# Two edits of a float32 post-norm transformer layer on one core: where ScalarE's copies of turned blocks stand beside its exponentials, and a 64-row feed-forward tile laid out over the whole TensorE array

## The chip, the cores and the metric

The kernel runs on one NeuronCore of one Trainium2 chip. The number that counts is the device time of one execution in microseconds (us). A core has five engines that run side by side, each through its own instruction list: PE (TensorE), DVE (VectorE), ACT (ScalarE), POOL (GpSimd) and SP (SyncE). They meet at semaphores that the kernel counts up and waits for by hand. There is no scheduler: the order of each engine's list is the order of the Python calls.

## The reference, cut to what matters

```python
B, T, C = 2, 1024, 1024                      # attention, 32 heads of 32, float32
q, k, v = (proj(wq), proj(wk), proj(wv))
q, k = _apply_rope(q, sin, cos), _apply_rope(k, sin, cos)
scores = jnp.where(causal, jnp.einsum('bnth,bnsh->bnts', q, k) * (1.0 / math.sqrt(h)), -jnp.inf)
out = jnp.einsum('bnts,bnsh->bnth', jax.nn.softmax(scores, axis=-1), v)
x = _layernorm(x + jnp.einsum('btc,dc->btd', out.transpose(0, 2, 1, 3).reshape(B, T, C), wo))
...
Wg, Wu, Wd = (codebook[idx].reshape(idx.shape[0], -1) for idx in (idx_gate, idx_up, idx_down))
h = jax.nn.silu(jnp.einsum('bsh,ih->bsi', x, Wg)) * jnp.einsum('bsh,ih->bsi', x, Wu)   # I = 2752
x = _layernorm(x + jnp.einsum('bsi,hi->bsh', h, Wd))
```

The feed-forward weights are not given: they are looked up in a codebook of 16384 entries of 8 numbers.

## The kernel before, in words

The kernel goes through five stages: projections of queries, keys and values (to about 680 us), attention (to about 1565 us), output projection with the first normalisation (to about 2190 us), the feed-forward part (to about 6700 us), and the last normalisation.

**Attention.** There are 16 passes (8 groups of 4 heads, 2 batches), 8 rounds each. A round takes two heads and two blocks of 128 query rows, a short one (block 0, 1, 2 or 3) and a long one (block 7, 6, 5 or 4), as the table `BLOCKS` pairs them: the rounds cycle through (0, 7), (1, 6), (2, 5), (3, 4). So a round has four score rows, numbered e = 0, 1 (short, both heads) and e = 2, 3 (long). On PE a round u is: short scores, long scores (`scores`, L311 and, for the mask, L314); the turns (transposes, `turn`, L327) of round u-1's probabilities, in six pieces of at most four 128x128 blocks, numbered j = 0, 1 (short heads), j = 2, 3 (long, first head), then the weighing with the values of round u-2 (`weigh`, L346), then pieces j = 4, 5 (long, second head). Two PSUM banks hold the turned pieces in alternation, so piece j waits until ACT has copied piece j-2 (`turns_copied`). DVE finds row maxima (L908), ACT takes exponentials (`exponent`, L615), DVE normalises (L915) and copies the weighed output (L923); ACT also copies the turned pieces to SBUF (`copy_turned`, L624). Among other things, the weighing waits for the exponentials 0 and 1 of round u and for all six copies of round u-2; the long scores wait for all four exponentials of the round before; each exponential waits for its row maximum. The order on ACT is written in `attention_round` (L626):

```python
exponent(i, u, 0); exponent(i, u, 1)
copy_turned(i, u - 1, 0); copy_turned(i, u - 1, 1)
exponent(i, u, 2)
copy_turned(i, u - 1, 2); copy_turned(i, u - 1, 3)
exponent(i, u, 3)
copy_turned(i, u - 1, 4); copy_turned(i, u - 1, 5)
```

**The feed-forward part.** The inner dimension 2752 is 21 tiles of 128 and one of 64 (`HALF`), which goes first, as step 0. A step is 32 slots. In each slot PE does one codebook lookup for a later tile (16 one-pass matmuls against one-hot columns, `look_up`, L420), and then `ffn_matmul` issues three matmuls of the current tile: first 64 of gate and up (`gate_up`, L450: per group t of 512 tokens 8 for gate, then 8 for up), then 32 of down (`down`, L468). Each of these is a float32 matmul, which the trace records as two (x6 is three matmuls). Every fourth slot adds four folding matmuls (`fold`, L431). DVE makes five of a slot's eight one-hot tiles (L996), picks out of the looked-up sums (L1003), multiplies silu(gate) by up (`hidden`, L980) and adds each down product to the residual stream in SBUF (`add`, L988); ACT makes the other three one-hot tiles in two operations each (L757, L761), applies Silu (`gate`, L740) and issues the loads of codes (L743, L744). The one-hot tiles have one buffer each: tile k for slot s+1 is written once PE has used tile k of slot s. Down products go through a ring of three PSUM banks: product d waits for the add of d-3.

In step 0 the tile of 64 takes half an array in both parts: gate and up have 64 output columns each, down has a contraction of 64 rows. ACT takes the Silu at slots 2, 7, 13 and 18.

## Time and profile before

| what | value |
|---|---|
| median of 3 runs (lowest, highest) | 6821.02 us (6820.23, 6821.85) |
| the profiled execution's own time | 6826.36 us |
| its span | 6824.5 us |
| busy: PE, DVE, POOL, ACT | 6664.1 (98%), 4664.4 (68%), 4936.2 (72%), 3779.4 us (55%) |
| PE L420 lookups, x12288 | 3259.1 us busy |
| PE L450 gate and up, x2816 records | 1297.0 us busy |
| PE L468 down, x1408 records | 652.7 us busy |
| chain that ended last, PE's share | 75% |

The profiled execution is 1.9 us longer than its span (what lies before and after the first and last instruction) and 5.3 us above the median. Busy time of PE is a modelled figure, since its matmuls are pipelined; the distance between the starts of two groups is the sounder measure of what a group costs, and is what the sums here use. A line such as "[0.65 <-ACT arena L624]" says that the engine sat idle for 0.65 us just before the row and that ACT's instruction of line 624 ended the wait.

### The profile page before, as it was taken

How to read it: one execution, taken by the hardware profiler on the slowest of the kernel's cores; microseconds unless marked ns; L12 is line 12 of the kernel's file. 1: busy time of each engine (PE TensorE's matmuls, PEld its weight loads, DVE VectorE, ACT ScalarE, POOL GpSimd, SP SyncE). 2: the span in 40 equal slices, each digit the busy share in tenths (PEclk: the TensorE clock that was granted, in tenths of full speed). 3: DMA queues.
4: the chain of work that ended last, by engine and by line, in shares of the span. 5: the costliest groups of instructions: out<-in, count | busy, mean ns of one | idle time of the engine just before them, and what ended most of it. 6: DMA issues, size and time to landing. Idle time of an engine off the chain costs nothing.

```text
span 6824.5 us, 120862 instructions
## 1 busy us (share of the span) xinstructions
PE 6664.1 (98%) x29648; PEld 4072.6 (60%) x29648; DVE 4664.4 (68%) x11403; ACT 3779.4 (55%) x6691; POOL 4936.2 (72%) x5188
## 2 busy tenths in 40 slices
PE   9999899999999999999999999999999999999998
PEld 3444565666666566666666666666666666666664
DVE  3320788887777667777677776777667776677765
ACT  0000787886666555555555555555555555556553
POOL 7777777777777777777777777777777777777771
PEclk9999999999999999999999999999999999999999
DMA  4232222233333333333333333333333333233331
GB/s 138 65 87 49 53 59 54 53 84 72 82 80 76 66 72 66 74 73 73 74 70 72 75 73 71 68 74 73 74 68 73 75 72 74 66 74 72 74 68 64
DMA packets 480031, 491.50 MB, mean 72 GB/s; under 512 B 228672, under 2 KB 349248, under 8 KB 472896
## 3 DMA queue, kind: packets, MB, share of 16 engines
q10 hardware_dynamic: 298720, 425.47, 22.3%
q0 software_dynamic: 165888, 21.57, 7.8%
q1 hardware_dynamic: 14688, 36.48, 1.4%
q8 instruction: 239, 3.92, 0.2%
q14 instruction: 496, 4.06, 0.2%
HBM read 426.34 MB, written 56.72 MB: 71 GB/s over the span
## 4 chain that ended last, share of the span: by engine, by line
PE 75%; ACT 1%; issue 1%; DVE 0%; ACTq 0%; DMA 0%; DVEq 0%
PE ps L420 41%; PE ps L450 18%; PE ps L468 9%; PE ps L395 3%; PE ps L431 3%; PE ps L437 1%; ACT onehot L757 0%; ACT onehot L761 0%; PE ps L406 0%; PE ps L543 0%; DVE small L1045 0%; DVE onehot L996 0%; ACT arena L852 0%; DMA arena<-code_low 0%; DVE small L1048 0%
## 5 line engine op out<-in xcount | busy, mean ns | idle before, releaser
L209 POOL DMA_INDIRECT raw<-in_codebook_dram,idx_sb x5184 | 4936.0, 952 | 1758.1 <-DMA raw<-in_codebook_dram,idx_sb 1556.3
L996 DVE TENSOR_SCALAR_CACHE_REDUCE onehot<-arena,small 128x512 fp32r<-128x512 f32 x3845 | 2622.9, 742 | 1095.7 <-PE ps L420 1054.2
L420 PE MATMUL ps<-onehot,table 128*128 128x512 f32 x12288 | 3259.1, 416 | 28.2 <-ACT onehot L761 18.5
L420 PEld LDWEIGHTS ps<-onehot,table 128*128 128x128 f32 x12288 | 2289.5, 188 | 908.8 <-issue 380.5
L757 ACT ACTIVATE onehot<-arena,small 128x512 fp32r<-128x512 f32 x2307 | 1496.6, 713 | 1170.2 <-PE ps L420 1045.2
L761 ACT ACTIVATE onehot<-onehot,small 128x512 fp32r<-128x512 f32 x2307 | 1487.3, 708 | 0.0
L450 PE MATMUL ps<-big,arena 128*128 128x512 f32 (+1 forms) x2816 | 1297.0, 597 | 0.0
L450 PEld LDWEIGHTS ps<-big,arena 128*128 128x128 f32 (+1 forms) x2816 | 514.2, 187 | 595.0 <-issue 569.6
L1003 DVE SCALAR_TENSOR_TENSOR picked<-arena,small,ps 128x512 f32<-128x512 f16 x768 | 572.0, 745 | 161.9 <-PE ps L431 146.5
L468 PE MATMUL ps<-arena 128*128 128x512 f32 (+1 forms) x1408 | 652.7, 599 | 1.8 <-ACT arena L733 1.2
L908 DVE TENSOR_REDUCE small<-ps 128x1 f32<-128x384 f32 (+7 forms) x512 | 373.9, 751 | 297.8 <-PE ps L314 294.9
L988 DVE TENSOR_TENSOR big<-ps,big 128x512 f32<-128x512 f32 x704 | 486.2, 691 | 114.4 <-PE ps L468 104.2
L615 ACT ACTIVATE arena<-ps,small 128x384 f32<-128x384 f32 (+7 forms) x512 | 380.3, 745 | 176.6 <-DVE small L908 167.6
L277 PE MATMUL ps<-big,arena 128*128 128x512 f32 x1024 | 442.4, 595 | 16.8 <-DMA big<-in_xT_dram 16.8
L468 PEld LDWEIGHTS ps<-arena 128*128 128x128 f32 (+1 forms) x1408 | 255.2, 190 | 287.7 <-issue 264.1
L327 PE MATMUL ps<-id_sb,arena 128*128 128x128 f32 x2304 | 334.0, 281 | 74.5 <-ACT arena L624 72.9
L277 PEld LDWEIGHTS ps<-big,arena 128*128 128x128 f32 x1024 | 195.5, 191 | 262.8 <-issue 262.8
L624 ACT COPY arena<-ps 128x512 f32<-128x512 f32 (+3 forms) x768 | 330.6, 488 | 10.3 <-PE ps L327 9.9
L327 PEld LDWEIGHTS ps<-id_sb,arena 128*128 128x128 f32 x2304 | 247.0, 141 | 138.6 <-ACT arena L624 124.1
L996 DVE DVE_READ_ACCUMULATOR onehot<-arena,small 128x1 f32 x3845 | 318.6, 83 | 0.0
L740 ACT ACTIVATE arena<-ps 128x512 f32<-128x512 f32 (+1 forms) x88 | 52.5, 597 | 480.2 <-PE ps L450 480.2
L915 DVE TENSOR_SCALAR arena<-arena,small 128x384 f32<-128x384 f32 (+7 forms) x512 | 275.5, 538 | 18.1
(72 smaller groups left out, 2719.5 us busy)
## 6 DMA issues: line engine op xcount, KB each, us to landing
arena<-code_low ACTq DMA_DIRECT2D x770, 256.0 KB
arena<-code_high ACTq DMA_DIRECT2D x770, 128.0 KB
raw<-in_codebook_dram,idx_sb POOLq DMA_INDIRECT x5184
gathered_units<-raw SPq DMA_DIRECT2D x39, 512.0 KB, 3.3
arena<-gathered_units ACTq DMA_DIRECT2D x19, 1024.0 KB
queries_keys<-arena ACTq DMA_DIRECT2D x16, 1024.0 KB, 4.0
arena<-queries_keys ACTq DMA_DIRECT2D x32, 512.0 KB
big<-queries_keys ACTq DMA_DIRECT2D x32, 512.0 KB
```

What stands on the lines that cost most here:

```text
L209: pool.indirect_dma_start(raw[:, s, n, :], None, codebook, bass.IndirectOffsetOnAxis(ap=idx_sb[:, s, n:n + 1], axis=0), engine_sem=describ ...
L277: last = mm(ps[:, 4 * m + 2 * b + h, :], w_sb[:, m, k, :], big1[:, k, b * T + h * N:b * T + (h + 1) * N], start=(k == 0), stop=(k == KT - 1))
L327: last = nc.tensor.transpose(ps[:, 6 + j % 2, (s % 4) * P:(s % 4 + 1) * P], probs_of[u % 2][2 * o + n][:, s * P:(s + 1) * P], id_sb[:, :])
L420: last = mm(ps[:, 4 + s % 2, :], table[:, k, c, :], onehot[:, k, :], start=(k == 0 and c == 0), stop=(k == KLO - 1 and c == PIECES - 1))
L450: one = mm(ps[0:ni, 2 * (t % 2) + m, :], w_rep[:, m, k, 0:ni], big1[:, k, t * N:(t + 1) * N], start=(k == 0), stop=(k == CS - 1))
L468: mm(ps[:, d % banks, :], d_rep[0:ni, h * P:(h + 1) * P], hT[0:ni, t * N:(t + 1) * N], start=True, stop=True).then_inc(down_done, 1)
L615: act.activation(probs_of[u % 2][e][:, 0:L], src[:, 0:L], ACT.Exp, bias=negmax[:, e:e + 1], scale=1.0, accum_out=rowsum[:, e:e + 1]).then_ ...
L757: act.activation(onehot[:, k, :], lo_sb[:, s % 2, :], ACT.Abs, bias=kp_sb[:, k:k + 1], scale=-1.0).then_inc(distance_done, 1)
L761: act.activation(onehot[:, k, :], onehot[:, k, :].bitcast(F32), ACT.Relu, bias=one_sb, scale=-1.0).then_inc(near_ready, 1)
L988: dve.tensor_tensor(big2[:, h, cols], ps[:, d % banks, :], before[:, h, cols], ALU.add).then_inc(y_added, 1)
L996: dve.tensor_scalar(onehot[:, k, :], lo_sb[:, s % 2, :], kp_sb[:, k:k + 1], None, ALU.is_equal, ALU.add, accum_out=hits[:, k:k + 1]).then_ ...
L1003: dve.scalar_tensor_tensor(picked[:, s % QUAD, :], hi_sb[:, s % 4, :], hi_row_sb, ps[:, 4 + s % 2, :], ALU.is_equal, ALU.mult).then_inc(ma ...
```

## The change

It makes two edits that have nothing to do with each other.

**In attention** ACT's order in a round becomes: exponentials 0 and 1, copies 0 to 3, exponentials 2 and 3, copies 4 and 5. Nothing else there is touched.

**In step 0** the half tile is laid out over the whole array. Gate and up become one matmul of 128 output columns, gate in partitions 0 to 63 of the PSUM bank and up in 64 to 127, so there are 32 instead of 64. Silu moves gate's rows to partitions 64 to 127 of `hT`; DVE multiplies twice, once into partitions 0 to 63 and once in place, so that `hT` holds the tile twice. ACT copies the turned down weights twice too (one more instruction), and down's matmuls take their 64 rows from the lower and the upper half in turn. A slot now carries two matmuls instead of three (64 in 32 slots), the adds follow the same count, and the Silus stand at slots 4, 8, 12 and 16. Later steps are unchanged.

```diff
@@ tensor
-                one = mm(ps[0:ni, 2 * (t % 2) + m, :], w_rep[:, m, k, 0:ni], big1[:, k, t * N:(t + 1) * N],
+                one = mm(ps[:, 2 * (t % 2) + m, :], w_rep[:, m, k, :], big1[:, k, t * N:(t + 1) * N],
                          start=(k == 0), stop=(k == CS - 1))
...
-                mm(ps[:, d % banks, :], d_rep[0:ni, h * P:(h + 1) * P], hT[0:ni, t * N:(t + 1) * N],
+                rows = half_rows(h % 2) if isinstance(step, int) and step == 0 else slice(0, P)
+                mm(ps[:, d % banks, :], d_rep[rows, h * P:(h + 1) * P], hT[rows, t * N:(t + 1) * N],
                    start=True, stop=True).then_inc(down_done, 1)
...
+                if isinstance(step, int):
+                    if n < CS * NT:
+                        gate_up(step, n // CS, 0, n % CS)
+                    else:
+                        down(step, n - CS * NT)
...
-                    for n in range(3 * s, 3 * s + 3):
-                        ffn_matmul(step, ni, n)
+                    beside = 2 if isinstance(step, int) else 3
+                    for n in range(beside * s, beside * s + beside):
+                        ffn_matmul(step, n)
@@ scalar, attention_round
                 if turned:
-                    copy_turned(i, u - 1, 0)
-                    copy_turned(i, u - 1, 1)
+                    for j in range(4):
+                        copy_turned(i, u - 1, j)
                 if scored:
                     exponent(i, u, 2)
-                if turned:
-                    copy_turned(i, u - 1, 2)
-                    copy_turned(i, u - 1, 3)
-                if scored:
                     exponent(i, u, 3)
@@ scalar, step 0
+                out_rows, in_rows = ((half_rows(1), half_rows(0)) if isinstance(step, int) and step == 0
+                                     else (slice(0, P), slice(0, P)))
+                act.activation(hT[out_rows, t * N:(t + 1) * N], ps[in_rows, 2 * (t % 2), :], ACT.Silu
+                               ).then_inc(silu_ready, 1)
...
+                gates = (4, 8, 12, 16) if isinstance(step, int) and step == 0 else (2, 7, 13, 18)
@@ vector, hidden
+                if isinstance(step, int) and step == 0:
+                    rows = half_rows(1)
+                    dve.tensor_tensor(hT[half_rows(0), cols], hT[rows, cols], ps[rows, 2 * (t % 2), :],
+                                      ALU.mult).then_inc(short_ready, 1)
+                    dve.wait_ge(short_ready, t + 1)
+                    dve.tensor_tensor(hT[rows, cols], hT[rows, cols], ps[rows, 2 * (t % 2), :],
+                                      ALU.mult).then_inc(hT_ready, 1)
```

The first place is ACT's list in attention, the round of the blocks (2, 5); line 615 (629 in the changed kernel) is an exponential, line 624 (638) a copy of a turned piece. Before:

```order
L615 ACTIVATE arena,small<-ps,small 128x384
L622 REGISTER_ALU
L624 COPY arena<-ps 128x256
L622 REGISTER_ALU
L624 COPY arena<-ps 128x256
L612 REGISTER_ALU
L615 ACTIVATE arena,small<-ps,small 128x768
L622 REGISTER_ALU
L624 COPY arena<-ps 128x512
L622 REGISTER_ALU
L624 COPY arena<-ps 128x384
L612 REGISTER_ALU
```

Now:

```order
L629 ACTIVATE arena,small<-ps,small 128x384
L636 REGISTER_ALU
L638 COPY arena<-ps 128x256
L636 REGISTER_ALU
L638 COPY arena<-ps 128x256
L636 REGISTER_ALU
L638 COPY arena<-ps 128x512
L636 REGISTER_ALU
L638 COPY arena<-ps 128x384
L626 REGISTER_ALU
L629 ACTIVATE arena,small<-ps,small 128x768
L626 REGISTER_ALU
```

The copies of 512 and 384 columns (pieces 2 and 3) have moved ahead of the exponential over 768 columns.

The second place is PE's list in step 0, at the end of gate and up and the beginning of down; line 420 (427) is a lookup, 431 (438) a fold, 450 (457) gate and up, 468 (476) down. Before:

```order
L420 MATMUL ps<-onehot,table 128x512 x16
L431 MATMUL ps<-picked,arena 32x512 x4
L450 MATMUL ps<-big,arena 64x512 x3
L420 MATMUL ps<-onehot,table 128x512 x16
L450 MATMUL ps<-big,arena 64x512
L468 MATMUL ps<-arena 128x512 x2
L420 MATMUL ps<-onehot,table 128x512 x16
L468 MATMUL ps<-arena 128x512 x3
```

Now:

```order
L457 MATMUL ps<-big,arena 128x512 x2
L427 MATMUL ps<-onehot,table 128x512 x16
L438 MATMUL ps<-picked,arena 32x512 x4
L476 MATMUL ps<-arena 128x512 x2
L427 MATMUL ps<-onehot,table 128x512 x16
L476 MATMUL ps<-arena 128x512 x2
```

Gate and up go to all 128 partitions, two matmuls stand in each slot, and down begins with slot 16 instead of inside slot 21.

## Rows read from the trace of the kernel before

**Rows 1.** Waits of all engines, 690 to 1556 us (attention): total us, times, longest us
```profile
ACT arena L615 <- DVE small L908: 167.6, 224, 7.0
PE ps L327 <- ACT arena L624: 71.7, 158, 1.6
```

**Rows 2.** Timeline of PE: start us, us, line, operation, count, idle before and its releaser
```profile
728.79 1.14 PE L327 MATMUL ps<-id_sb,arena 128*128 128x128 f32 x8 [0.65 <-ACT arena L624]
...
1050.41 1.09 PE L327 MATMUL ps<-id_sb,arena 128*128 128x128 f32 x8 [0.25 <-ACT arena L624]
...
1051.43 1.30 PE L346 MATMUL ps<-arena 128*32 128x128 f32 x36
...
1053.38 1.15 PE L327 MATMUL ps<-id_sb,arena 128*128 128x128 f32 x8 [0.65 <-ACT arena L624]
...
1541.40 0.85 PE L327 MATMUL ps<-id_sb,arena 128*128 128x128 f32 x6 [0.68 <-ACT arena L624]
```

**Rows 3.** Timeline of ACT in the same round
```profile
1051.75 1.01 ACT L615 ACTIVATE arena<-ps,small 128x896 f32<-128x896 f32 x1 [1.23 <-DVE small L908]
...
1052.75 1.06 ACT L624 COPY arena<-ps 128x512 f32<-128x512 f32 x2
```

**Rows 4.** Timeline of ACT, the end of the round before it
```profile
1045.31 1.12 ACT L615 ACTIVATE arena<-ps,small 128x1024 f32<-128x1024 f32 x1
...
1047.04 1.14 ACT L615 ACTIVATE arena<-ps,small 128x1024 f32<-128x1024 f32 x1
...
1048.14 0.77 ACT L624 COPY arena<-ps 128x512 f32<-128x512 f32 x2
...
1049.10 0.47 ACT L615 ACTIVATE arena<-ps,small 128x256 f32<-128x256 f32 x1 [0.19 <-DVE small L908]
```

**Rows 5.** Windows: step 0 of the feed-forward part, busy us of each engine, clock, DMA share
```profile
2190.00:2412.60 222.60, 221.91 (x768) 122.06 (x768) 155.81 (x387) 127.44 (x203) 161.62 (x172) 0.99 0.30 63
```

**Rows 6.** Timeline of PE in step 0: gate and up, down, and the start of step 1
```profile
2196.32 2.79 PE L450 MATMUL ps<-big,arena 128*64 128x512 f32 x6
...
2237.16 2.79 PE L450 MATMUL ps<-big,arena 128*64 128x512 f32 x6
...
2239.88 3.94 PE L420 MATMUL ps<-onehot,table 128*128 128x512 f32 x16
...
2243.75 1.50 PE L450 MATMUL ps<-big,arena 128*64 128x512 f32 x3
...
2354.86 2.84 PE L468 MATMUL ps<-arena 64*128 64x512 f32 x6
...
2357.63 1.66 PE L420 MATMUL ps<-onehot,table 128*128 128x512 f32 x6
...
2412.63 0.73 PE L420 MATMUL ps<-onehot,table 128*128 128x512 f32 x2
```

**Rows 7.** Timeline of PE in the output projection: two whole-array matmuls between lookups
```profile
1974.32 4.22 PE L420 MATMUL ps<-onehot,table 128*128 128x512 f32 x16
...
1978.38 1.88 PE L395 MATMUL ps<-big 128*128 128x512 f32 x4
...
1979.69 4.23 PE L420 MATMUL ps<-onehot,table 128*128 128x512 f32 x16
```

**Rows 8.** Timeline of PE in attention: a pair of score matmuls in two row strips
```profile
1007.23 1.13 PE L311 MATMUL ps<-arena 32*128 32x512 f32 x4
...
1008.29 0.28 PE L314 MATMUL ps<-arena 128*128 128x128 bf16 x2
```

**Rows 9.** Timeline of DVE in one slot of step 0's down part
```profile
2351.86 0.74 DVE L996 TENSOR_SCALAR_CACHE_REDUCE onehot<-arena,small 128x512 fp32r<-128x512 f32 x1
...
2355.20 0.74 DVE L1003 SCALAR_TENSOR_TENSOR picked<-arena,small,ps 128x512 f32<-128x512 f16 x1
...
2356.02 0.69 DVE L988 TENSOR_TENSOR big<-ps,big 128x512 f32<-128x512 f32 x1
...
2356.88 0.69 DVE L988 TENSOR_TENSOR big<-ps,big 128x512 f32<-128x512 f32 x1 [0.17 <-PE ps L468]
```

More of the change, by code:

```diff
@@ L439, in turn_weights, with gate_up @@
                 last.then_inc(w_turned, 1)
-            def gate_up(step, ni, t, m, k):
+            def gate_up(step, t, m, k):
                 if k == 0 and m == 0:
@@ L453, in gate_up, with down @@
                     one.then_inc((gate_done, up_done)[m], 1)
-            def down(step, ni, d, banks=3):
+            def down(step, d, banks=3):
                 t, h = divmod(d, CS)
@@ L458, in down @@
                     if isinstance(step, int):
-                        pe.wait_ge(d_ready, 1 + step // NTILE)
+                        pe.wait_ge(d_ready, 2 + step // NTILE)
                     else:
@@ L549, in _ @@
                     for h in range(CS):
-                        down(NTILE, P, t * CS + h, 2)
+                        down(NTILE, t * CS + h, 2)
                 if t:
@@ L729, in take, with turned, gate @@
                 act.copy(dst.rearrange("p (h c) -> p h c", h=2), ps[:, 6:8, :]).then_inc(taken, 1)
-            def turned(count, ni, bank):
+            def turned(count, rows, bank):
                 act.wait_ge(turn_done, count)
-                act.copy(d_rep[0:ni, :].rearrange("p (h c) -> p h c", h=2),
-                         ps[0:ni, bank:bank + 2, :]).then_inc(d_ready, 1)
-            def gate(step, ni, t):
+                for out_rows in rows:
+                    act.copy(d_rep[out_rows, :].rearrange("p (h c) -> p h c", h=2),
+                             ps[0:out_rows.stop - out_rows.start, bank:bank + 2, :]).then_inc(d_ready, 1)
+            def gate(step, t):
                 act.wait_ge(gate_done, step * NT + (t + 1))
@@ L772, in lookup_step @@
                             take(unit - 1, d_rep)
-                    if s in (2, 7, 13, 18):
-                        gate(step, ni, (2, 7, 13, 18).index(s))
+                    if s in gates:
+                        gate(step, gates.index(s))
                     if s == 20 and not (isinstance(step, int) and step == 0):
@@ L818, in _ @@
                     if k == 1 and q == 0:
-                        turned(1, HALF, 2)
+                        turned(1, (half_rows(0), half_rows(1)), 2)
                     if k and q == 2:
@@ L825, in _ @@
             copy_x1(SB - 1)
[L827 removed]
+            lookup_step(0, 3)
             with act.Fori(1, NTILE - 1) as step:
[L829 to L830 removed]
+                lookup_step(step, step + 3)
+            lookup_step(NTILE - 1, NLOOK - 1)
             act.wait_ge(lo_in[1], NLOOK * SLOTS * 8 + 16)
@@ L837, in _ @@
             for t in range(NT):
-                gate(NTILE, P, t)
+                gate(NTILE, t)
             act.wait_ge(down_done, NTILE * 32)
-            turned(2, P, 4)
+            turned(2, (slice(0, P),), 4)
             for k in range(SB + 1):
@@ L1004, in pick, with ffn_work @@
                                          ALU.is_equal, ALU.mult).then_inc(masked, 1)
-            def ffn_work(step, ni, s):
-                for n in range(3 * s, 3 * s + 3):
-                    if n < 2 * CS * NT:
-                        if n % (2 * CS) == 2 * CS - 1:
-                            hidden(step, ni, n // (2 * CS))
+            def ffn_work(step, s):
+                beside, each = (2, CS) if isinstance(step, int) else (3, 2 * CS)
+                for n in range(beside * s, beside * s + beside):
+                    if n < each * NT:
+                        if n % each == each - 1:
+                            hidden(step, n // each)
                     else:
-                        add(step, n - 2 * CS * NT)
+                        add(step, n - each * NT)
             def look_up(unit, s):
@@ L1034, in _ @@
                         norm(k)
-            lookup_step(0, HALF, 3)
+            lookup_step(0, 3)
             with dve.Fori(1, NTILE) as step:
-                lookup_step(step, P, step + 3)
+                lookup_step(step, step + 3)
             for t in range(NT):
-                hidden(NTILE, P, t)
+                hidden(NTILE, t)
             def measure(k):
```

44 lines of the change are left out of this document (21 added, 23 removed).

## The prediction

> **What bounds the kernel now.** I read the busy times first: PE is at work nearly all the time, so a gain has to come from work that PE no longer does, or from a wait of PE that goes. Then I read the waits over attention. The largest wait on PE's matmuls there is for ACT's copies of turned pieces: 71.7 us in 158 waits [rows 1]. The timeline of one period of four rounds says which copies. Most of these waits stand ahead of piece 2, which waits for the first copies of the round (the wait of 0.25 us at 1050.41) [rows 2]; the change leaves those first copies where they are. One wait per period stands behind the weighing, ahead of piece 4, and only in the round of the blocks (1, 6): the weighing runs from 1051.43 to 1052.73, the turns start at 1053.38, 0.65 us idle. I count 32 of these in attention, 21.7 us in all; the first full one and the last are shown [rows 2]. Piece 4 waits for copy 2. In ACT's timeline copies 2 and 3 start at 1052.75, just behind exponential 2, which ran from 1051.75 and had itself waited 1.23 us for its row maximum [rows 3]. Piece 2, which copy 2 reads, was turned well before: its turns started at 1050.41.
>
> For the other edit the windows show that PE is busy for 221.9 of the 222.6 us of step 0 [rows 5], so its matmuls are the path there. From the first gate matmul (2196.32) to the first lookup of step 1 (2412.63) it is 216.3 us [rows 6].
>
> **Attention, part by part.** Nothing is added or removed: each of the 128 rounds has copies 2 and 3 ahead of exponential 2. In the round of (1, 6), piece 2 is four blocks of the eight that start at 1050.41 and take 1.09 us; it is done about 0.6 us in, at 1051.0. Copies 2 and 3 take 1.06 us together [rows 3], so copy 2 is done near 1051.6, long before the weighing ends at 1052.73. The 0.65 us wait goes whole: 32 times, 21.7 us. Exponential 2 now starts near 1052.1 instead of 1051.75. It is late by some 0.3 us, but exponential 3 no longer stands behind two copies; it ends earlier than before.
>
> What is late next? ACT does the same work in another order, so the end of its round moves only if ACT idles somewhere new. The tightest round is (0, 7): exponentials of 1.12 and 1.14 us with copies between them, the last two copies of 0.77 us ending at 1048.91, and the next round's exponential 0 at 1049.10 after 0.19 us of waiting for a row maximum [rows 4]. From 1045.31 to 1048.91 ACT does not idle. In the new order it starts there with copy 2, whose piece is ready about 0.1 us after 1045.31. That is within the 0.19 us. In the other rounds the wait before exponential 0 or 2 is longer; ACT waits 167.6 us for row maxima over attention [rows 1], about 1.3 us a round. I take 20.5 us of the 21.7, bounds 0 and 24 (some more could come since exponential 3 and its normalisation finish earlier).
>
> **Step 0, gate and up.** Before, three half-width matmuls take 2.72 us (2237.16 to 2239.88) and the lookup behind them 3.87 us (to 2243.75) [rows 6]: a slot of 6.59 us, 0.907 us per matmul. The nearest row for the new slot is the output projection, whose matmuls have the same shape (128 rows, 128 columns, 512 moving): two take 1.31 us (1978.38 to 1979.69), the lookup behind such a group 4.06 us (1974.32 to 1978.38) [rows 7]. So the new slot is 5.37 us.
>
> **Step 0, down.** Before, three take 2.77 us (2354.86 to 2357.63) [rows 6]. DVE's adds follow them 0.86 us apart (2356.02 to 2356.88) [rows 9], so 0.19 us of the 2.77 is the change of shape. The new pairs use the lower and the upper 64 rows, with different banks. The trace shows no such pair on 64 rows; it shows two float32 score matmuls on two different strips of 32 rows, and they take 1.06 us together (1007.23 to 1008.29) [rows 8], where two in a row would take 1.72. I take 1.06 + 0.19 = 1.25 us a pair, since it is the same mechanism one size down. Bounds: 1.72 + 0.19 = 1.91 (they do not overlap) and 0.86 + 0.19 = 1.05 (they overlap whole). The Trainium skill (TensorE: Matmul & The Clock Gate, Part 3: Packing small matmuls) gives a pack of tiles the time of one matmul and about 4 ns for each further tile; by it a pair would cost what the lower bound does and the sum would be 3 us better. The row speaks against it: 1.06 and not 0.86 us.
>
> **The sum for step 0**, from the first gate matmul to step 1: before, 31 lookups of 3.87 (120.0), 64 gate and up matmuls of 0.907 (58.0) and 32 downs of 0.923 (29.5) make 207.6; the remaining 8.7 us of the 216.3 are folds and a few waits for ACT, and I leave them. Now: 16 groups of 1.31 (21.0), 16 lookups behind them of 4.06 (65.0), 16 pairs of 1.25 (20.0), 15 lookups behind pairs of 3.87 (58.1): 164.1, and with the 8.7 it is 172.8. The difference is 43.5 us.
>
> Is DVE or ACT the bound then? In a down slot DVE does five one-hot tiles (2351.86 to 2355.20, 3.34 us), a pick (0.82) and two adds of 0.69: 5.54 us [rows 9]. PE's slot is 3.87 + 1.25, with a fold of about 1 us in every fourth: 5.37 on average. DVE is the longer by 0.17 us, 2.7 us over 16 slots. But one-hot tiles are written more than a slot ahead, so DVE can fall behind by a few us before PE notices. I charge 1 us. The second multiplication of `hidden` (0.69 us, four times) and ACT's added copy of the down weights (about 1 us, once) lie in gate slots or in the projection, where DVE has over a slot to spare; if that cover were gone they would cost 4 us together. The Silus at slots 4, 8, 12 and 16 find gate already finished; before they held up ACT's one-hot tiles a little, which is some of the 8.7. So step 0 gives 42.5 us, bounds 31 and 47.
>
> **The forecast**: 20.5 + 42.5 = 63 us off. The profiled execution would go from 6826.4 to 6763.4; it stands 5.3 us above the median, so the median goes from 6821.0 to 6758 us.
>
> **The rivals.** (1) *Attention gives nothing.* The exponentials 2 and 3 that come later delay the next round as much as the missing wait gains, for instance because the 0.19 us of slack in (0, 7) is too little. Against it stand the 167.6 us of ACT's idle time; for it, that these engines are coupled tightly. Time: 6821.0 - 42.5 = 6778.5. (2) *The pairs do not overlap*, since each carries its own semaphore step and the second a wait: 1.91 instead of 1.25 us, 16 times, 10.6 us back: 6768.5. (3) *DVE paces down.* If its adds stay 0.86 us apart as now, its slot is 3.34 + 0.82 + 1.72 = 5.88 us against PE's 5.37, 8 us over 16 slots: about 6765. The Trainium skill has this as a rule (TensorEngine Tiling (Array Packing), Performance Considerations, PSUM Bottleneck): packing speeds up TensorE but not the evacuation of PSUM, which may become the bottleneck. (4) *Slower than before.* Copies 2 and 3, 0.77 to 1.06 us together, now stand ahead of exponential 2. If that delay were carried on, through exponential 3, copies 4 and 5 and exponential 0 into the long scores of the next round, in each of 128 rounds, it would cost some 0.9 x 128 = 115 us, and the kernel would take 6821 + 115 - 42.5 = 6894. It decides from 0.33 us carried per round on (42.5 us). Against it: exponential 3 follows directly, and all of ACT's work after it comes at the time it came before; only ACT's idle time counts, and there is some in each round. (5) *More than forecast*: whole overlap in down (3 us) and the earlier exponential 3 shortening other rounds too, 10 us more: 6748.
>
> **How the numbers follow.** A measurement of this kernel can tell about 0.2%, 13.6 us, from no change. Chances: forecast 0.56 (its own range 6753 to 6764), rival 1 0.13, rival 2 0.10, rival 3 0.12, rival 4 0.03, rival 5 0.06. All but rival 4 are faster by far more than 13.6 us; step 0 alone is three times that. I leave 0.02 for no change (attention giving back most of step 0's gain) and 0.03 for slower. The range goes from 6744 to 6780, which takes in rivals 1, 2, 3 and 5.
>
> **What would show it.** Right: behind the weighing in the rounds of (1, 6) no wait for a copy; PE's wait for copies in attention down from 71.7 to about 50 us; attention 20 us shorter; gate slots of 5.4 us; a down pair of about 1.25 us between the lookups; step 0 from 216 to about 174 us; later steps as before. Wrong: new waits of the long scores on exponential 3, or of DVE's normalisation on exponential 2; a pair of 1.9 us; DVE without any idle time in down while PE waits for one-hot tiles; gate slots near 6 us.

## The result and the profile after

| | before | after |
|---|---|---|
| median (lowest, highest), 6 runs each | 6821.1 us (6820.23, 6822.56) | 6788.0 us (6781.07, 6794.32) |
| ratio to before, 95% interval | | 0.9951 [0.9938, 0.9964] |
| the profiled execution | 6826.36 us | 6794.32 us |

The kernel is 33.1 us faster. I had forecast 63 us, with a range from 6744 to 6780 us, so the time lies outside the range, on the side of a smaller gain. The runs of after are also spread over 13 us, these six of before over 2.3 us (later sets of before, of 7 to 13 runs, over 6.5 to 7.5 us).

**The two edits did in their places what was forecast, and a little more.** In attention the waits behind the weighing are gone. Here are the waits of 690 to 1541 us in the trace of after (the columns are those of [rows 1]; PEld is the load of a matmul's weights):

```profile
ACT arena L629 <- DVE small L922: 79.8, 103, 6.5
...
PE ps L334 <- ACT arena L638: 49.8, 126, 1.1
PEld ps L318 <- DVE big L937: 14.8, 59, 0.5
```

PE waits for copies 126 times instead of 158, and 49.8 instead of 71.7 us. The round of the blocks (1, 6) shows how. PE's timeline of after:

```profile
1013.72 1.09 PE L334 MATMUL ps<-id_sb,arena 128*128 128x128 f32 x8 [0.25 <-ACT arena L638]
...
1014.74 1.30 PE L353 MATMUL ps<-arena 128*32 128x128 f32 x36
1015.97 1.09 PE L334 MATMUL ps<-id_sb,arena 128*128 128x128 f32 x8
1017.23 0.91 PE L318 MATMUL ps<-arena 32*128 32x384 f32 x4 [0.17 <-DVE big L937]
```

and ACT's:

```profile
1014.41 1.07 ACT L638 COPY arena<-ps 128x512 f32<-128x512 f32 x2 [0.58 <-PE ps L334]
1015.37 1.02 ACT L629 ACTIVATE arena<-ps,small 128x896 f32<-128x896 f32 x1
...
1016.57 1.01 ACT L629 ACTIVATE arena<-ps,small 128x896 f32<-128x896 f32 x1
```

The turns of piece 4 follow the weighing (1014.74, 1.30 us) without a wait; in [rows 2] 0.65 us lay between. ACT has copied pieces 2 and 3 while PE still weighed, and the two exponentials come behind. A small new wait is there: the weight loads of the next scores wait up to 0.5 us for DVE's copy of the weighed output (L937), 59 times and 14.8 us in all; of the matmuls themselves 11 wait (0.17 us in the row). The first lookup of step 0 starts at 2165.23 us instead of 2190.07, 24.8 us earlier.

PE's timeline of step 0 in after, for [rows 6]:

```profile
2165.23 5.43 PE L427 MATMUL ps<-onehot,table 128*128 128x512 f32 x16 [1.10 <-ACT big L715]
...
2171.59 1.98 PE L457 MATMUL ps<-big,arena 128*128 128x512 f32 x4
...
2182.46 1.88 PE L457 MATMUL ps<-big,arena 128*128 128x512 f32 x4
2183.78 4.24 PE L427 MATMUL ps<-onehot,table 128*128 128x512 f32 x16
2187.86 1.88 PE L457 MATMUL ps<-big,arena 128*128 128x512 f32 x4
...
2269.75 4.31 PE L427 MATMUL ps<-onehot,table 128*128 128x512 f32 x16
2273.99 1.13 PE L476 MATMUL ps<-arena 64*128 64x512 f32 x4
...
2306.12 1.13 PE L476 MATMUL ps<-arena 64*128 64x512 f32 x4
2307.18 3.92 PE L427 MATMUL ps<-onehot,table 128*128 128x512 f32 x16
2311.03 1.13 PE L476 MATMUL ps<-arena 64*128 64x512 f32 x4
...
2342.70 4.00 PE L427 MATMUL ps<-onehot,table 128*128 128x512 f32 x16
```

A gate slot is 5.40 us (2182.46 to 2187.86), a down pair 1.06 us (2306.12 to 2307.18) and the lookup behind it 3.85 us. From the first gate matmul to step 1 it is 171.1 us (2171.59 to 2342.70) instead of 216.3, so step 0 gives 45.2 us. DVE's timeline in a down slot of after, for [rows 9]:

```profile
2303.60 1.30 DVE L1010 TENSOR_TENSOR big<-ps,big 128x512 f32<-128x512 f32 x2
...
2308.12 0.76 DVE L1025 SCALAR_TENSOR_TENSOR picked<-arena,small,ps 128x512 f32<-128x512 f16 x1
2308.78 1.30 DVE L1010 TENSOR_TENSOR big<-ps,big 128x512 f32<-128x512 f32 x2
2309.98 0.75 DVE L1018 TENSOR_SCALAR_CACHE_REDUCE onehot<-arena,small 128x512 fp32r<-128x512 f32 x1
```

The two adds take 1.30 us together and the next one-hot tile starts right behind them. A slot of DVE is 5.18 us (2303.60 to 2308.78), and from the first down slot on DVE's timeline shows no idle time. PE's weight loads wait for its one-hot tiles, first in PEld's timeline and then in the waits of the down slots (2256 to 2343 us):

```profile
2269.75 1.22 PEld L427 LDWEIGHTS ps<-onehot,table 128*128 128x128 f32 x6 [0.76 <-DVE onehot L1018]
```

```profile
PEld ps L427 <- DVE onehot L1018: 14.2, 25, 0.8
```

In the first four down slots this shows in PE's lookups, which take 4.12 to 4.24 us (2269.75 to 2273.99) instead of 3.85 us, 1.2 us in all. Behind them PE and DVE go at the same pace.

**At step 1 after is 69.9 us ahead** (2412.63 - 2342.70). At the end it is 32.0 us ahead in the profiled executions. What is missing is lost around one wait of PE, in step 19. PE's timeline of after there:

```profile
6328.23 2.85 PE L427 MATMUL ps<-onehot,table 128*128 128x512 f32 x10
...
6373.53 2.93 PE L427 MATMUL ps<-onehot,table 128*128 128x512 f32 x6 [42.45 <-ACT onehot L775]
```

PE stands for 42.45 us in the middle of a lookup, for a one-hot tile of ACT. Why does ACT not make it? ACT's timeline of after (ACTq is its queue of issued transfers):

```profile
6323.39 0.34 ACTq L757 DMA_DIRECT2D arena<-code_low  x1
6324.18 0.34 ACTq L758 DMA_DIRECT2D arena<-code_high  x1
...
6370.40 0.39 ACTq L726 DMA_DIRECT2D arena<-gathered_units  x1
...
6370.92 1.94 ACT L771 ACTIVATE onehot<-arena,small 128x512 fp32r<-128x512 f32 x3 [47.81 <-SPq L243]
```

After 6324.5 its next instruction is the load of two stored units, the gate and up weights of step 20 (L726). Gate's and up's weights do not come through lookups on PE. For steps 2 to 20, and for three units besides, POOL gathers them straight from the codebook, a unit in 128 indirect transfers (64 for the first), 5184 in all from the start of the kernel to near its end (L209 before, L216 after); SP stores each finished unit, and ACT loads two units a step again. The load waits for SP's store. SP's timeline of after:

```profile
6367.42 0.34 SPq L238 DMA_DIRECT2D gathered_units<-raw  x1
```

The same two instructions before, first SP's store:

```profile
6368.19 0.34 SPq L231 DMA_DIRECT2D gathered_units<-raw  x1
```

then ACT's load:

```profile
6401.09 0.39 ACTq L716 DMA_DIRECT2D arena<-gathered_units  x1
```

Before, the unit was stored 33 us ahead of the load (6368.19 against 6401.09), of which the store's own landing takes some 3 us (6367.42 to 6370.40 in after). **So before had 30 us to spare here.** After reaches the load some 77 us earlier (6324.5 against 6401.1), but the store comes within 1 us of its time before. Neither edit touches the gathers. Why is it this load that waits? In before the load one step earlier had 142 us to spare (stored at 6042.50, loaded at 6187.16): two units take POOL longer than a step takes PE, so the slack shrinks from step to step. The next place with little of it is the last unit, which PE turns itself: 52 us before, by its turn at 6747.60, the last gather at 6693.59 and the 2.4 us that its data took in a run below (e8). The last gather before:

```profile
6693.59 0.94 POOL L209 DMA_INDIRECT raw<-in_codebook_dram,idx_sb  x1 [0.31 <-issue]
```

and after:

```profile
6690.38 0.94 POOL L216 DMA_INDIRECT raw<-in_codebook_dram,idx_sb  x1 [0.30 <-issue]
```

The chain that ended last says the same; here of after, where PE had 75% before:

```profile
DMA 69%; issue 23%; PE 6%; POOLq 1%; POOL 1%; DVE 0%; ACT 0%; ACTq 0%; DVEq 0%; SPq 0%
```

The folds of both traces can be counted off against each other, 192 in each, and their distance is how far after is ahead. The last fold ahead of the wait and the first behind it, before:

```profile
6401.24 1.06 PE L431 MATMUL ps<-picked,arena 128*32 128x512 f32 x8
...
6427.78 1.06 PE L431 MATMUL ps<-picked,arena 128*32 128x512 f32 x8
```

and the same two after:

```profile
6324.95 1.06 PE L438 MATMUL ps<-picked,arena 128*32 128x512 f32 x8
...
6395.91 1.07 PE L438 MATMUL ps<-picked,arena 128*32 128x512 f32 x8
```

After is 76.3 us ahead at the first and 31.9 us at the second. So the place costs 44.4 us: 42.45 us of waiting, and 1.9 us because PE works at its lower clock for 4 us behind it (the rows stand in the last section). From there to the end nothing changes, 32.0 us. The 6.4 us between step 1 (69.9) and the wait (76.3) are not the edits': the profiled execution of before stands 5.3 us above its median, and e16 below, a version of the kernel before in which neither edit stands, gains 7.9 us on it over the same stretch.

### The profile page after: what moved, and what is told of

Same layout as the page of the kernel before. It is cut to its first block, busy times and chain, and to the rows that moved or that the text cites. A ratio compares the mean times of both kernels' runs of the same rounds, so it can differ in the third digit from the quotient of the medians.

```text
span 6792.5 us, 120734 instructions
## 1 busy us (share of the span) xinstructions
PE 6614.0 (97%) x29584; PEld 4064.1 (60%) x29584; DVE 4662.6 (69%) x11407; ACT 3789.3 (56%) x6692; POOL 4927.0 (73%) x5188
## 4 chain that ended last, share of the span: by engine, by line
DMA 69%; issue 23%; PE 6%; POOLq 1%; POOL 1%; DVE 0%; ACT 0%; ACTq 0%; DVEq 0%; SPq 0%
DMA raw<-in_codebook_dram,idx_sb 69%; PE ps L427 2%; PE ps L457 2%; POOLq L215 1%; PE ps L476 1%; POOL raw L216 1%; PE ps L557 0%; PE ps L438 0%; DVE small L1068 0%; ACT arena L866 0%; DMA out_dram<-arena 0%; PE ps L444 0%; DMA gathered_units<-raw 0%; POOLq L204 0%; ACT onehot L771 0%
## 5 line engine op out<-in xcount | busy, mean ns | idle before, releaser
L216 POOL DMA_INDIRECT raw<-in_codebook_dram,idx_sb x5184 | 4926.8, 950 | 1764.1 <-DMA raw<-in_codebook_dram,idx_sb 1556.5
L457 PE MATMUL ps<-big,arena 128*128 128x512 f32 x2752 | 1268.3, 597 | 0.0
L457 PEld LDWEIGHTS ps<-big,arena 128*128 128x128 f32 x2752 | 510.5, 189 | 571.8 <-issue 543.7
L476 PE MATMUL ps<-arena 128*128 128x512 f32 (+1 forms) x1408 | 639.0, 599 | 2.1 <-ACT arena L744 1.2
L284 PE MATMUL ps<-big,arena 128*128 128x512 f32 x1024 | 442.2, 595 | 16.4 <-DMA big<-in_xT_dram 16.4
L334 PE MATMUL ps<-id_sb,arena 128*128 128x128 f32 x2304 | 332.6, 281 | 51.6 <-ACT arena L638 49.8
L284 PEld LDWEIGHTS ps<-big,arena 128*128 128x128 f32 x1024 | 195.4, 191 | 262.4 <-issue 262.4
```

The costliest lines, as they stand in the source:

```text
L216: pool.indirect_dma_start(raw[:, s, n, :], None, codebook, bass.IndirectOffsetOnAxis(ap=idx_sb[:, s, n:n + 1], axis=0), engine_sem=describ ...
L284: last = mm(ps[:, 4 * m + 2 * b + h, :], w_sb[:, m, k, :], big1[:, k, b * T + h * N:b * T + (h + 1) * N], start=(k == 0), stop=(k == KT - 1))
L334: last = nc.tensor.transpose(ps[:, 6 + j % 2, (s % 4) * P:(s % 4 + 1) * P], probs_of[u % 2][2 * o + n][:, s * P:(s + 1) * P], id_sb[:, :])
L457: one = mm(ps[:, 2 * (t % 2) + m, :], w_rep[:, m, k, :], big1[:, k, t * N:(t + 1) * N], start=(k == 0), stop=(k == CS - 1))
L476: mm(ps[:, d % banks, :], d_rep[rows, h * P:(h + 1) * P], hT[rows, t * N:(t + 1) * N], start=True, stop=True).then_inc(down_done, 1)
```

## The experiments

**Theory A**: the stream of gathers has an end that the edits do not move, and the path of PE meets it in the last steps. Whatever PE gains beyond the stream's slack is given back there. **Its rivals**: the wait of 42 us is an accident of the profiled execution and the missing gain lies elsewhere in PE's list; or each edit simply gives less than its place in the trace shows. The first separates the edits, the second shortens the stream.

**The first four runs** fell into another regime, in which the kernel before takes 12966.9 us (12956 to 12982 in 14 runs). They are the two halves of the change by themselves, and both kernels with a shorter stream. The half with attention alone and the half with step 0 alone are the change's diff without its other part:

```diff
@@ e1, e6: before, with attention_round as in the change
-                    copy_turned(i, u - 1, 0)
-                    copy_turned(i, u - 1, 1)
+                    for j in range(4):
+                        copy_turned(i, u - 1, j)
...
-                    copy_turned(i, u - 1, 2)
-                    copy_turned(i, u - 1, 3)
...
@@ e2, e7: after, with attention_round as before
-                    for j in range(4):
-                        copy_turned(i, u - 1, j)
+                    copy_turned(i, u - 1, 0)
+                    copy_turned(i, u - 1, 1)
...
+                    copy_turned(i, u - 1, 2)
+                    copy_turned(i, u - 1, 3)
...
```

The shorter stream makes 124 gathers for a unit instead of 128, but for the first unit. It leaves out the last 4 of the 128 index columns of each of these units, whose weights are zero instead:

```diff
@@ e3 and e5 (on after), e4 (on before)
+GC = P - 4
...
+            pool.memset(raw[:, :, GC:P, :], 0.0).then_inc(tail_zero, 1)
...
-            gather_unit(0, 1, P, 16, 0, CS * CS)
+            gather_unit(0, 1, GC, 16, 0, CS * CS)
```

> The kernel before with only the new order of ACT's copies in attention. Theory A (POOL's stream of gathers is the next bound: the load of up's weights for step 20 stood at 6401 us before, its unit was stored at 6368 us, so about 29 us can be gained ahead of it and no more): attention gives its 24.8 us, all of it under the 29 us, so 6821.1 - 24.8 = 6796, and PE has no wait of tens of us late in the feed-forward part. Theory B (the reordered attention loses time elsewhere, later in the kernel, whatever the gathers do): under half of the 24.8 us arrives, 6809 us or more. Theory C (the two edits share one fixed loss of 37 us, for instance in a loop that both shift): 6821 or more.

> The changed kernel with the old order of the copies: the edit of step 0 alone. Theory A: step 0 gives 45 us by the trace, the gathers let only about 29 to 33 us through, so about 6789 to 6792 and one wait of PE of some 15 us near 6360 us, behind ACT's wait for the stored unit. The two edits alone then add up to 54 to 57 us where both together give 33. Theory B (nothing caps it): 6776 us and no such wait.

> The changed kernel with 124 instead of 128 gathers in each unit but the first (the last 4 of 128 columns of indices are left out, their codebook entries are zero), so that POOL's stream ends about 40 x 4 x 1.25 = 200 us earlier; PE, ACT and DVE have the same instructions. Theory A: the wait of 42 us is gone and the whole 70 us arrive: 6821 - 70 = 6751 us, and its runs lie closer together than the 13 us of the changed kernel's. Theory B (the 37 us were lost on PE, DVE or ACT): within 5 us of the changed kernel's 6788.

> The kernel before with the same shorter gathers (4 of 128 columns left out): the control for the run on the changed kernel. Theory A: the gathers had 29 us to spare in the kernel before, so nothing changes: 6821 us, within 3 us. If the gathers already cost something before, through the DMA engines they share with the loads of codes, it is faster by that much.

Measured: 12955.7 us, ratio 0.999 [0.998, 1.0]; 12918.1 us, 0.9961 [0.9947, 0.9975]; 12691.6 us, 0.9785 [0.9768, 0.9801]; and 12754.3 us, 0.9833 [0.9816, 0.9849]. The numbers expected do not apply to this regime. The windows of the first show it (columns as in [rows 5]; the clock is the third number from the end):

```profile
0.00:7150.00 7150.00, 2066.93 (x6794) 864.66 (x6794) 622.11 (x1253) 462.64 (x1080) 4779.53 (x5037) 0.55 0.11 17
7150.00:12955.00 5805.00, 5546.52 (x22854) 3477.60 (x22854) 4053.05 (x10150) 3354.34 (x5611) 142.84 (x151) 0.98 0.22 63
```

As long as POOL gathers (its last gather starts at 7346.7 us in this run), the other engines do a fraction of their work: up to 7150 us PE ran 6794 of its 29648 matmul records. Behind the last gather all of them go at their usual pace. What follows for theory A is little: the shorter stream gives the kernel before 212.6 us there. Between e3 and e4, with the stream shortened in both, the change is worth 62.8 us; how much of it comes without a shorter stream was not measured in this regime, and which part of the list gains it was not read.

**The shorter stream on after, again.**

> The changed kernel with 124 instead of 128 gathers in each unit but the first (4 of 128 columns of indices left out), again, since the four runs before this were on a chip where the kernel before takes 12967 us. If this chip runs the kernel before in 6821 us: theory A (the gathers' stream caps the gain) expects 6751 us and no wait of PE of tens of us; theory B (the 37 us were lost on PE, DVE or ACT) expects about 6788 us.

Measured: 6751.7 us (6749.93 to 6752.81), ratio 0.9895 [0.9878, 0.9911]. With 3% fewer gathers and PE's list as it was, the gain is 70.3 us, the 69.9 that after has in hand at step 1. The last gather starts at 6490.9 us, no wait of PE in the last steps is above 3.3 us, and the runs are within 3 us of each other. The chain that ended last:

```profile
PE 75%; ACT 1%; issue 1%; DVE 0%; DMA 0%; ACTq 0%; DVEq 0%
```

It is PE's again. Theory A stands, and the rivals fall: PE's list was not changed. One doubt is left here. The shorter stream also leaves out DMA work, and its control, the same stream on the kernel before (e4), was measured only in the other regime. The runs e8, e15 and e16 below answer it, since they leave no gather out.

**The two halves, again.**

> Attention's edit alone, on a chip that runs the kernel before in 6821 us. Theory A (the gathers cap the sum at about 29 us of head start): the 24.8 us stay under the cap and arrive whole, 6796 to 6797 us, no wait of PE of tens of us. Theory B (some share of any gain is lost, about half as in the changed kernel): 6809 us.

> Step 0's edit alone. Theory A: 45 us of head start meet a cap of 29 to 33 us, so 6788 to 6792 us, with one wait of 12 to 18 us on PE near 6350 us; alone it is worth as much as both edits together. Theory B (half of any gain is lost): 6798 us. No cap: 6776 us.

Attention alone: 6796.9 us (6795.86 to 6797.64), ratio 0.9964 [0.9951, 0.9976], 24.7 us faster. The waits of PE for copies over attention in its trace:

```profile
PE ps L327 <- ACT arena L624: 49.1, 126, 0.8
```

This is the whole local gain (24.8 us), as theory A expected, and it fits into the 30 us of slack. Step 0 alone: 6783.3 us (6779.47 to 6789.65), 0.9949 [0.9932, 0.9965], 38.3 us faster of the 45.2 it gains locally. Here the expectation of 6788 to 6792 us was missed. The gain is less than the local one, as the theory wants, but 5 us better than the cap that I had worked out from one trace of after, and PE's wait was far shorter than the 12 to 18 us expected. In its profiled execution PE waited only this long for the same unit:

```profile
6360.50 1.84 PE L427 MATMUL ps<-onehot,table 128*128 128x512 f32 x4 [3.16 <-ACT onehot L779]
```

and its stream of gathers ended earlier, by the view of their source line (duration min, median and max in ns; first and last start in us):

```profile
L216 POOL DMA_INDIRECT raw<-in_codebook_dram,idx_sb x5184: 938/944/3194, 3.6 to 6677.4; - x200
```

6677.4 us, where after had 6690.4. The end of the stream is not the same in each run: in the five traces with the same gathers it lies at 6693.6 (before), 6690.4 (after), 6689.3 (e6), 6677.4 (e7) and 6680.0 us (e8). The profiled execution of after is the slowest of its six, that of e7 the fastest of its four, which fits. The runs of after spread by 13 us and those of step 0 alone by 10, those of attention alone, which stays inside the slack, by 2 us. So the cap is no single number, and the 30 us of one trace are good to some 10 us. Alone the two edits give 24.7 + 38.3 = 63.0 us, together 33.1: they do not add, since both draw on the same slack.

**Asking less of the stream.** If the long wait is for the second of two units that one load takes, then loading them apart helps: gate's unit at slot 20 as now, up's at slot 26, just ahead of where PE turns it.

```diff
-            def load_gate_up(u):
-                act.wait_ge(unit_ready, u + 2)
-                act.dma_start(w_raw, units[bass.ds(u, 2)].rearrange("m p f -> p m f")).then_inc(gu_in, 16)
+            def load_one(u, m, done):
+                act.wait_ge(unit_ready, u + 1)
+                act.dma_start(w_raw[:, m, :], units[bass.ds(u, 1)].rearrange("m p f -> p (m f)")).then_inc(done, 16)
...
-                            load_gate_up(step * 2 - 1)
+                            load_one(step * 2 - 1, 0, gu_in)
+                    if s == 26 and not isinstance(step, int):
+                        load_one(step * 2, 1, up_in)
...
@@ tensor
+                        if r == 2:
+                            pe.wait_ge(up_in, step * 16)
```

> The changed kernel with the load of gate's and up's stored weights split: gate at slot 20 as before, up with its own wait at slot 26, and PE waits for it ahead of up's turn in slot 27. Theory A: the unit that is late is up's of the last such pair, needed six slots (about 40 us) later now, so the wait of 42 us shrinks to a few us; then the next need of the stream decides, the last down unit, whose gathers end near 6692 us: PE would come to it at about 6680 us, so 20 to 25 of the 42 us are won, 6763 to 6768 us. If the wait is not that of up's unit, nothing changes: 6788 us.

Measured: 6766.8 us (6763.65 to 6770.34), ratio 0.9923 [0.9906, 0.9939], as expected, with all gathers as they were. Of the 42 us nothing is left at step 19. The rest is now at the very last unit:

```profile
6682.31 1.97 PE L552 MATMUL ps<-id_sb,raw 128*128 128x128 f32 x8 [10.41 <-DMA raw<-in_codebook_dram,idx_sb]
```

PE waits 10.41 us for the last gathers themselves.

**A faster stream?** POOL has two gathers outstanding and waits for the one before the last. The edit lets it have three.

```diff
-AHEAD = 2
+AHEAD = 3
```

> The changed kernel with POOL allowed three gathers not yet described instead of two (one constant). POOL waits 0.30 us ahead of nearly each gather for the description of an earlier one, 1556 us in all. If that wait sets the pace of 1.25 us a gather, the stream becomes up to 0.3 us a gather faster, ends hundreds of us earlier, and the kernel takes about 6751 us; if the describing itself is the pace, nothing changes: 6788 us.

Measured: 6763.3 us (6761.71 to 6764.18), 0.9916 [0.9899, 0.9932], between the two values. The gathers by their source line in after:

```profile
L216 POOL DMA_INDIRECT raw<-in_codebook_dram,idx_sb x5184: 938/944/3193, 3.6 to 6690.4; - x200
```

and with three ahead:

```profile
L216 POOL DMA_INDIRECT raw<-in_codebook_dram,idx_sb x5184: 938/944/3200, 4.6 to 6659.6; - x200
```

The median step from one gather to the next stays at 1.25 us. What changed are the long steps: 52 of over 2 us (217 us in all) instead of 63 (267 us). The other steps are 18 us longer in all. The stream ends 30.8 us earlier than in after; against all five traces with two outstanding (6677.4 to 6693.6) it is 18 to 34 us. PE still waits 10.00 us at 6342.66.

**Both together**, on after, and as a control on before:

> The changed kernel with up's stored weights loaded on their own at slot 26 and three gathers ahead, a third time, for a chip that runs the kernel before in about 6821 us. Theory A: no wait for the stream is left and the whole 70 us arrive, 6751 to 6753 us. If three ahead costs something on the DMA engines, 6757 us or more.

> The two additions on the kernel before, for a chip that runs it in about 6821 us: 6820 to 6822 us, since the kernel before had 29 us to spare against the gathers. If it is faster by more, the 70 us of the version with everything are not the edits' alone.

On after it takes **6749.6 us** (6748.51 to 6751.19), ratio 0.9896 [0.9879, 0.9912]: 70.5 us faster than before, with nothing left out of the computation, and the fastest version of this study that computes everything. Its chain that ended last is PE's again, with the same shares as that of e5, and its stream ends at 6658.8 us. On before the same two edits give 6817.6 us (6814.98 to 6821.88), 0.9994 [0.9985, 1.0004]: no difference that can be told. They are worth 38.4 us behind the change and nothing that can be told ahead of it. This was tried twice more, in runs that fell into the regime of the first four (before 13024.3 and 13021.7 us):

> The changed kernel with both: up's stored weights loaded on their own at slot 26, and three gathers ahead. Each alone left one wait of 10 us on PE: the last down unit with the split, up's stored unit with three ahead. Together the stream ends near 6660 us, ahead of the 6680 us at which PE comes to the last down unit, and up's unit is needed 40 us later: no such wait is left and the whole 70 us arrive, 6751 to 6753 us. If three ahead had cost something on the DMA engines that the waits hid, 6757 us or more.

> The same two additions on the kernel before, the control. It has 29 us to spare against the gathers, so neither is worth anything there: 6821 to 6822 us. If they are faster by themselves, the 70 us would not be the edits' alone.

> The changed kernel with up's stored weights loaded on their own at slot 26 and three gathers ahead, again, on a chip that runs the kernel before in about 6821 us. Theory A: no wait for the stream is left and the whole 70 us arrive, 6751 to 6753 us. If three ahead costs something on the DMA engines, 6757 us or more.

> The same two additions on the kernel before, again, the control: 6821 to 6822 us, since it had 29 us to spare against the gathers. If it is faster, the 70 us are not the edits' alone.

There the version on after took 12980.5 us, 0.9968 [0.9956, 0.9979], and 12974.9 us, 0.9966 [0.9953, 0.9978]; on before 13029.4 us, 1.0003 [0.9993, 1.0012], and 13025.2 us, 1.0003 [0.9993, 1.0013]. They say nothing on the cap.

**Does the pair overlap, and what is that worth?** With the stream shortened, so that no cap hides it, all of down's matmuls of step 0 take their rows from the lower half (the values are the same in both halves):

```diff
-                rows = half_rows(h % 2) if isinstance(step, int) and step == 0 else slice(0, P)
+                rows = half_rows(0) if isinstance(step, int) and step == 0 else slice(0, P)
```

> The changed kernel with short gathers (4 of 128 columns left out), and down of step 0 taking its 64 rows from the lower half each time instead of from both in turn, so that a pair cannot overlap. Against the run with short gathers alone (6751.7 us): by the prediction's rows a pair goes from 1.06 us to 1.9 us between the lookups, 16 times, 10 to 13 us, 6762 to 6765 us. If DVE's adds and not PE set the pace of down (the rival of the prediction), hardly anything changes: 6752 to 6755 us.

> The changed kernel with short gathers (4 of 128 columns left out) and down of step 0 taking its rows from the lower half each time. Against 6751.7 us with short gathers alone: 6762 to 6765 us if PE sets the pace of down and pairs overlap only on two halves; 6752 to 6755 us if DVE's adds set the pace.

The first fell into the other regime (12768.4 us, 0.9806 [0.979, 0.9822]). The second took 6761.1 us (6759.42 to 6762.77), 0.9911 [0.9895, 0.9928], 9.4 us more than e5, which differs in that one line. This is 0.9 us under the first value expected, and far from the second. Its pair, by PE's timeline:

```profile
2297.78 1.98 PE L479 MATMUL ps<-arena 64*128 64x512 f32 x4
2299.69 3.92 PE L430 MATMUL ps<-onehot,table 128*128 128x512 f32 x16
```

1.91 us where after has 1.06. Sixteen pairs make 13.6 us by that. In the traces the way from the first gate matmul to step 1 is 183.3 us (2170.25 to 2353.57) against e5's 171.2 (2172.18 to 2343.33), 12.2 us more: the lookups behind the slower pairs take 3.85 us from the first slot on, since DVE now has the time for its one-hot tiles, and that gives back the 1.2 us of the first four slots. The rest of the way to 9.4 lies outside step 0, where these two executions differ without an edit: e17 is already 1.9 us earlier at its first gate matmul.

## Why the prediction was wrong

**The step that failed is the first: what bounds the kernel.** "PE is at work nearly all the time, so a gain has to come from work that PE no longer does, or from a wait of PE that goes" is true as far as it goes, but I took from it that all such work is a gain. I never asked what else has an end of its own. POOL was busy 72% of the span, so it did not look like a bound; yet it takes its next gather every 1.25 us, 5184 times, to 6693.6 of 6824.5 us, and nothing PE does makes that shorter. The slack between that stream and PE's path was 30 us, and it was to be read before: the store at 6368.2 against the load at 6401.1. No rival named it, and the low chance of everything above 6780 us was given without a reason. Had I read it, the cap would have been about 6821 - 30 = 6791, against 6788.0 measured; that the two agree to 3 us is in part luck, since the end of the stream moves by more than that between runs (e7). e5, e8, e9 and e15 show the cap by shortening the stream or asking less of it.

**Attention: the mechanism right, the term a little small.** All 32 waits behind the weighing went, as worked out, and ACT's later exponentials delayed nothing that can be seen. Measured 24.8 us, forecast 20.5, upper bound 24. The waits for copies fell by 21.9 us. The other 2.9 are not shown to be the edit's: after is already 0.5 us ahead at the first score matmul, and at the first fold behind attention e16 and e7, with attention as before, stand 1.7 us later and 0.9 us earlier than before does. Rivals 1 and 4 are wrong (e6: 24.7 us faster).

**Step 0, gate and up: right.** 5.40 us a slot, forecast 5.37.

**Step 0, down: the term mis-sized by 0.19 us a pair.** The pair takes 1.06 us, forecast 1.25. The overlap is that of [rows 8]; the change of shape that I had added, 0.19 us, is not paid in a pair. Sixteen times that is 3.0 us. In e17, where the pair stays on one half, it is: 1.91 us, the prediction's upper bound. The rule of the Trainium skill (TensorE: Matmul & The Clock Gate, Part 3: Packing small matmuls) would give little more than 0.86 us; the runs show 1.06 with overlap and 1.91 without. So rival 2 is wrong. Its pair of 1.91 us was right, and what no overlap costs was measured: 12.2 us in step 0, 9.4 us of the kernel's time.

**DVE: rival 3 right in kind, wrong in size.** DVE has no idle time in down and PE's weight loads wait for its one-hot tiles, which is one of the signs that I had named against me. But its adds come in one go of 1.30 us and not 0.86 us apart, since DVE reaches them when both products are long done (2308.78, the pair at 2306.12). Its slot is 5.18 us, not 5.54 or 5.88. PE's own slot, by e17 less the 0.85 us of the slower pair, is 5.17 us on average with its folds, so DVE is the longer by hardly anything. The waits cost PE the 1.2 us of the first four slots and 0.1 us in each four behind them, so the 1 us that I charged was about right. The rule of the Trainium skill (TensorEngine Tiling (Array Packing), Performance Considerations, PSUM Bottleneck) holds here in kind: with the pairs packed, DVE sets the pace of down, at a price of some 1.5 us.

**The sum up to step 1** was 63 us forecast and 69.9 measured: 4.3 more in attention, and 2.7 in step 0, of which the pairs are 3.0. Rival 5 (6748 us) would have been the nearest without the cap; e15, with the cap moved away, measures 6749.6 and e5 6751.7. But the overlap in down was not whole (1.06 us, not 0.86), so that part of its reason was wrong. Of the signs that I had named for the forecast, "later steps as before" is the one that the trace of after contradicts.

## What to carry to other kernels

Before summing what leaves the busiest engine, list every other stream that has a pace of its own, and at the last places where the path meets it read how long ahead its data were ready: that slack is the cap of all gains together, however low the stream's busy share. Gains that draw on the same slack do not add (24.7 and 38.3 alone, 33.1 together), and an edit that is worth nothing before (e16) can be worth as much as the change behind it. Runs that spread wider, here 13 us instead of 2 to 8, are a hint that the bound has moved to such a stream, and no more than a hint. A slack read from one trace is as uncertain as the stream's end, here some 10 us.

## What the runs showed of the hardware

- The indirect gathers of this kernel start 1.25 us apart (median), with two outstanding and with three. With three there are fewer long pauses, 52 of over 2 us instead of 63, and the stream of 5184 gathers ends at 6659.6 instead of 6677.4 to 6693.6 us.
- Two float32 matmuls with 64 rows each take 1.06 us on different halves of the array and 1.91 us on the same half. A float32 matmul of 128 rows and 64 columns (0.907 us in step 0 before) takes longer than one of 128 by 128 (0.655 us in a pair of after). Part of it is a matter of where the time is booked: the lookup behind the narrow ones starts its next row after 3.87 us, that behind the wide ones after 4.08. With these 0.21 us added to the pair a wide one costs 0.76 us, still less than 0.907.
- PE's granted clock fell during its wait of 42 us and was still low when work came back. PE had done nothing since 6331.1. In the windows of after (the clock is the third number from the end; 0.50 is the 1.2 GHz level, 1.00 the 2.4 GHz level):

```profile
6331.00:6342.00 11.00, 0.08 (x1) 0.00 (x0) 1.72 (x6) 0.00 (x0) 8.34 (x9) 0.73 0.07 3
6342.00:6352.00 10.00, 0.00 (x0) 0.00 (x0) 0.00 (x0) 0.00 (x0) 5.49 (x6) 0.50 0.06 2
...
6373.50:6375.50 2.00, 1.97 (x5) 1.57 (x6) 0.00 (x0) 1.20 (x2) 1.49 (x2) 0.50 0.76 278
6375.50:6377.50 2.00, 2.00 (x5) 1.09 (x4) 0.75 (x1) 1.47 (x3) 1.39 (x3) 0.61 0.50 161
6377.50:6380.00 2.50, 2.50 (x9) 1.38 (x8) 1.94 (x3) 2.32 (x4) 1.89 (x3) 1.00 0.20 33
```

  The six matmuls behind the wait take 2.73 us (6373.53 to 6376.26), where the ten ahead of it took 2.85 (6328.23 to 6331.08). By the folds this costs 1.9 us. In e9 six matmuls take 2.73 us behind the wait of 10.00 us as well, at a granted clock of 0.50.
- There is a regime in which this kernel takes 12967 to 13024 us instead of 6821. PE, DVE and ACT crawl there until POOL's gathers are done (at 7346.7 us in e1, 7100.6 in e3 with its shorter stream) and run at their usual pace afterwards. Runs made together all fell into the same regime. Whether it belongs to a chip is not shown: by their numbers, chips 2 and 13 had runs in this regime (e1, e10) and runs in which before takes 6822 and 6820 us (e16, e15). The traces give no releaser within the kernel for most of the idle time; why the gathers go with a hold-up of the other engines there, and not elsewhere, stays open.
